# First loads, tanh and constants as ordered steps, and all orders laid down anew, in a two-layer gated cross-attention and mixture-of-experts kernel

## The reference

```python
x = x + tanh(g_xattn[0]) * L0_xattn(layernorm(x), ctx_768, ...)   # 8 heads of 64, softmax over 512 keys
x = x + tanh(g_ffn[0])   * L0_ffn(layernorm(x), ...)              # 16 heads of 8 over 256 keys + top-2 of 8 experts
x = x + tanh(g_xattn[1]) * L1_xattn(layernorm(x), ctx_768, ...)   # 16 heads of 8, softmax over 512 keys
x = x + tanh(g_ffn[1])   * L1_ffn(layernorm(x), ...)              # router, top-2 of 8 experts
```

## Time and profile before

| | before |
|---|---|
| median of 3 timed runs | 726.27 us (725.82 to 726.75) |
| the profiled execution | 733.98 us, span 732.2 us |
| mean granted clock of PE | 0.968 |
| busy share of PE, DVE, ACT, POOL | 91%, 70%, 55%, 53% |

### The profile page before, as it was taken

How to read it: one execution, slowest core, us unless ns; L and a number is a source line. 1 busy time by engine, 2 the same in 40 slices (tenths; PEclk the granted TensorE clock), 3 DMA queues, 4 the chain that set the end, 5 groups by cost and what they waited for, 6 DMA issues and landing times.

```text
span 732.2 us, 14403 instructions
## 1 busy us (share of the span) xinstructions
PE 666.7 (91%) x5766; PEld 347.3 (47%) x5766; DVE 515.4 (70%) x1018; ACT 402.4 (55%) x574; POOL 385.8 (53%) x535
## 2 busy tenths in 40 slices
PE   6898998998989899988999998999999999999984
PEld 4454554543445454543445454546445543544542
DVE  2505658698558965778868889777479979957636
ACT  1464556446734676426673586476744666376540
POOL 5465675781454547563538746573648625234041
PEclk9899999999898999989999999999999989999998
DMA  6040400511091010820145124240060031000000
GB/s 179 22 95 5 101 3 9 119 24 45 10 161 34 2 45 9 168 33 3 46 99 104 54 51 86 56 99 10 1 130 26 20 78 45 1 20 8 2 1 15
DMA packets 58338, 36.92 MB, mean 50 GB/s; under 512 B 4984, under 2 KB 56288, under 8 KB 58272
## 3 DMA queue, kind: packets, MB, share of 16 engines
q1 hardware_dynamic: 57728, 35.74, 22.2%
q10 hardware_dynamic: 544, 0.26, 0.1%
HBM read 21.07 MB, written 14.93 MB: 49 GB/s over the span
## 4 chain that ended last, share of the span: by engine, by line
PE 53%; DVE 26%; ACT 6%; POOL 5%; DMA 4%; issue 3%; SPq 1%; DVEq 0%; POOLq 0%; ACTq 0%
PE psum L878 7%; PE psum L730 6%; PE psum L743 5%; DVE mx8B L1225 5%; DVE mx8F L1220 5%; PE psum L834 5%; PE psum L866 4%; DVE mxA L1105 3%; PE psum L847 2%; PE psum L702 2%; PE psum L803 2%; PE psum L708 2%; ACT probB L996 2%; PE psum L815 2%; PE psum L761 1%
## 5 line engine op out<-in xcount | busy, mean ns | idle before, releaser
L1225 DVE TENSOR_REDUCE mx8B<-psum 128x2 f32<-128x1024 f32 x112 | 131.6, 1216 | 15.1 <-PE psum L847 14.2
L996 ACT ACTIVATE probB<-psum 128x1024 f32<-128x1024 f32 x112 | 110.7, 1028 | 25.5 <-PE psum L866 19.9
L953 ACT ACTIVATE probX<-psum 128x1024 f32<-128x1024 f32 x64 | 65.5, 1023 | 54.8 <-PE psum L734 54.2
L1105 DVE TENSOR_REDUCE mxA<-psum 128x2 f32<-128x1024 f32 x64 | 76.5, 1217 | 25.2 <-PE psum L714 24.9
L1220 DVE TENSOR_REDUCE mx8F<-psum 128x4 f32<-128x1024 f32 x56 | 66.2, 1219 | 21.9 <-PE psum L841 21.5
L730 PE MATMUL psum<-qA,kA 64*128 64x256 f32 x512 | 76.9, 393 | 1.0 <-ACT mrow L926 0.5
L996 ACT ACTIVATE probF<-psum 128x1024 f32<-128x1024 f32 x56 | 56.7, 1026 | 21.1 <-PE psum L866 17.8
L743 PE MATMUL psum<-probX,vX 128*64 128x256 f32 x512 | 63.8, 393 | 0.7 <-ACT probX L953 0.3
L1316 POOL TENSOR_TENSOR prodC<-prodC 128x256 f32<-128x256 f32 x28 | 20.3, 727 | 73.7 <-DVE prodC L1197 73.7
L878 PE MATMUL psum<-probB,v8B 128*9 128x256 f32 x896 | 56.0, 392 | 0.3 <-ACT probB L996 0.2
L1292 POOL TENSOR_TENSOR sums<-probX 128x512 f32<-128x512 f32 x32 | 40.6, 1267 | 21.4 <-ACT probX L953 21.3
(11 more groups left out here) (254 smaller groups left out, 1368.0 us busy)
## 6 DMA issues: line engine op xcount, KB each, us to landing
k8B<-k_dK SPq DMA_DIRECT2D x14, 384.0 KB, 6.8
k_dK<-partsK SPq DMA_DIRECT2D x7, 384.0 KB, 2.6
q8F<-q_dF SPq DMA_DIRECT2D x14, 192.0 KB, 4.3
k8F<-k_dF SPq DMA_DIRECT2D x14, 192.0 KB, 5.0
q8B<-q_dB SPq DMA_DIRECT2D x14, 192.0 KB, 4.0
k_dK<-partsK SPq DMA_DIRECT2D x7, 256.0 KB, 2.9
cTX<-in_ctxT SPq DMA_DIRECT2D x8, 192.0 KB, 2.6
cTK<-in_ctxT SPq DMA_DIRECT2D x8, 192.0 KB, 2.5
```

The lines of the kernel that those rows point to most:

```text
L953: nc.scalar.activation(prob[s][k % SLOTS[s]][:], ps, ACT.Exp, scale=float(XD) ** -0.5).then_inc(done["ACT"], 1)
L996: nc.scalar.activation(prob[s][(units * b + k) % SLOTS[s]][:], ps, ACT.Exp, scale=float(D8) ** -0.5).then_inc(done["ACT"], 1)
L1105: nc.vector.tensor_reduce(mxA[:, t, h:h + 65:64], ps.rearrange("p (i n) -> p i n", i=2), AX.X, ALU.max, negate=True).then_inc(drained, 1)
L1225: nc.vector.tensor_reduce(mx8[s][:, t, 2 * p:2 * p + 2], ps.rearrange("p (i n) -> p i n", i=2), AX.X, ALU.max, negate=True).then_inc(drain ...
```

## The change

The 25 loads that SP issued ahead of its list become steps `("X", "ld", 0, k)`, so that the table orders them among `xin` and `ctx`. The gates move from ACT's queue to SP's, and `wqx` and `wvx` from SP's to ACT's. The tanh becomes the step `th` of ACT's list. The two masked biases leave `sets` and become a step of their own, `bm`, with a semaphore of its own (`b_set`), for which only the steps of the last batch element wait. The planner's figures change: an entry of SP's queue now lands no earlier than those ahead of it have been served (`SERVE`), and no filler matmul is planned ahead of 12 us on its own clock (`FILL_FROM`). All five strings are new. The number of filler matmuls falls from 15 to 6; the rest of the instructions is the same.

```diff
-START = {"PE": 5.4, "DVE": 5.2, "ACT": 5.0, "POOL": 1.3, "SP": 9.0}
+START = {"PE": 5.4, "DVE": 5.2, "ACT": 4.0, "POOL": 1.3, "SP": .75}
+LOADS, FIRST_LOADS, LANDED = 25, 5, 9
+SERVE = {"sr": {"F": 4.6, "K": 5., "B": 2.2}, "sw": {"F": 2.6, "K": 2.1, "B": 1.3}, "ctx": {"X": .9, "K": .9}}
+FILL_FROM = 12.
...
-    "POOL": "dacebalffffffffggehijfafffjffffjjkggehlimajfnojffjfjffffkggheimjjjjkonfalfpfffffqqfqmggheqriojjfpnffjfjffakfflqq"
+    "POOL": "abdcmfgggaggggghhfimjgkggagkggkggklhhfijngapkkggkgkgglggohhfijknakkpgeklggggqogggmrhhifrnrjrspkqkgaoggkgggggrklm"
...
+    if b == 0:
+        for k in range(LOADS):
+            p.job("SP", "X", "ld", b, k, .46)
     plan_norm(p, "X", b, [("SP", "X", "xin", b, 0)], [("PE", "X", "qp", b - 1, 0)])
     if b == 0:
         p.job("POOL", "X", "pick", b, 0, 1.1)
-        p.job("POOL", "X", "bo", b, 0, 1.3)
+        p.job("ACT", "X", "th", b, 0, .2, ("SP", "X", "ld", 0, LANDED + 1))
+        p.job("POOL", "X", "bo", b, 0, 1.3, ("ACT", "X", "th", b, 0), ("SP", "X", "ld", 0, LANDED + 3))
         p.job("POOL", "K", "sets", b, 0, 9.8)
+        p.job("POOL", "F", "bm", b, 0, .65, ("SP", "X", "ld", 0, LOADS - 1))
...
+                if e == "SP" and key[2] != "ld":
+                    served = over[key] = max(over[key], served + SERVE.get(key[2], {}).get(key[1], .35))
...
-        warm[fill] = int(min(20, max(0., idle - IDLE) // WARM_UP)) if WARM else 0
+        warm[fill] = int(min(20, max(0., idle - IDLE) // WARM_UP)) if WARM and start > FILL_FROM else 0
...
+        first = [(loaded["graw"], graw[:, 0:2], a["g_xattn"].rearrange("(o n) -> o n", o=1).broadcast_to([P, 2])),
+                 (loaded["graw"], graw[:, 2:4], a["g_ffn"].rearrange("(o n) -> o n", o=1).broadcast_to([P, 2])),
+                 (loaded["bo"], bo["X"][:], a["boX"].rearrange("(o n) -> o n", o=1).broadcast_to([P, P])),
+                 (loaded["bo"], bo["B"][:], a["boB"].rearrange("(o n) -> o n", o=1).broadcast_to([P, P])),
+                 (loaded["wox"], wox[:], a["wox"])]
+        loads = first + [(w_loaded, dst, src) for dst, src in loads]
...
-            load_ctx("X", 0)
-            load_x(0)
-            engine.dma_start(wqx[:], a["wqx"]).then_inc(loaded["wqx"], 16)
-            engine.dma_start(wvx[:], a["wvx"]).then_inc(loaded["wvx"], 16)
...
+                elif name == "ld":
+                    which, dst, src = loads[k]
+                    engine.dma_start(dst, src).then_inc(which, 16)
...
-            act.wait_ge(loaded["graw"], 32)
-            nc.scalar.activation(gates[:], graw[:], ACT.Tanh).then_inc(tanh_done, 1)
+            engine.dma_start(wqx[:], a["wqx"]).then_inc(loaded["wqx"], 16)
+            engine.dma_start(wvx[:], a["wvx"]).then_inc(loaded["wvx"], 16)
...
+                if name == "th":
+                    act.wait_ge(loaded["graw"], 32)
+                    nc.scalar.activation(gates[:], graw[:], ACT.Tanh).then_inc(tanh_done, 1)
+                    continue
...
-                    act.wait_ge(k_set, K_SETS)
+                    act.wait_ge(b_set, 2)
...
+                elif name == "bm":
                     pool.wait_ge(w_loaded, W_LOADS)
                     for to, n in (("F", 0), ("B", 2)):
-                        engine.tensor_scalar(bqm[to][:], mask[:], bqn[:, n:n + 1], None, ALU.mult).then_inc(k_set, 1)
+                        engine.tensor_scalar(bqm[to][:], mask[:], bqn[:, n:n + 1], None, ALU.mult).then_inc(b_set, 1)
```

More of the change, by code:

```diff
@@ L133, in plan_x @@
 def plan_x(p, b):
-    p.job("SP", "X", "xin", b, 0, .4 if b else 0., ("DVE", "X", "xh", b - 1, 0), ("POOL", "X", "xb", b - 1, 0))
-    p.job("SP", "X", "ctx", b, 0, .4 if b else 0., ("PE", "X", "kp", b - 1, 1), ("PE", "X", "vp", b - 1, 1))
+    p.job("SP", "X", "xin", b, 0, .4, ("DVE", "X", "xh", b - 1, 0), ("POOL", "X", "xb", b - 1, 0))
+    p.job("SP", "X", "ctx", b, 0, .4, ("PE", "X", "kp", b - 1, 1), ("PE", "X", "vp", b - 1, 1))
+    if b == 0:
+        for k in range(LOADS):
+            p.job("SP", "X", "ld", b, k, .46)
     plan_norm(p, "X", b, [("SP", "X", "xin", b, 0)], [("PE", "X", "qp", b - 1, 0)])
@@ L270, in plan_k @@
     for k in range(2):
-        p.fill("DVE", 0, "K", "vv", b, k, .45, .33, [("SP", "K", "ctx", b, 0)], [("PE", "B", "pv8", b - 1, 3), ("POOL", "K", "sets", b, 0)])
+        p.fill("DVE", 0, "K", "vv", b, k, .45, .33, [("SP", "K", "ctx", b, 0), ("SP", "X", "ld", b, LOADS - 1)], [("PE", "B", "pv8", b - 1, 3), ("POOL", "K", "sets", b, 0)])
 def plan_b(p, b):
@@ L304, in slack @@
 def slack(key):
+    if key[:3] == ("SP", "X", "ld"):
+        return 4. * (key[4] == LOADS - 1)
     if key in (("SP", "X", "xin", 0, 0), ("SP", "X", "ctx", 0, 0)):
-        return 0.
+        return 4.
     return OUT if key[0] == "PE" else LAND[key[1:3]] if key[0] == "SP" else 0.
@@ L341, in schedule @@
     bank_free, bank_of, held = [0.] * BANKS, {}, [None] * BANKS
-    mode = 0
+    mode, served = 0, 0.
     over, before, warm = {}, {}, {}
@@ L575, in build @@
                       (we[s][:].rearrange("p (e n) -> p e n", e=NE), a["we" + s].rearrange("e k n -> k e n"))]
-        bias = [(bo[n][:], a["bo" + n].rearrange("(o n) -> o n", o=1).broadcast_to([P, P])) for n in "XB"]
-        W_LOADS = 16 * len(loads)
-        X_SETS, K_SETS = 3, 7
+        first = [(loaded["graw"], graw[:, 0:2], a["g_xattn"].rearrange("(o n) -> o n", o=1).broadcast_to([P, 2])),
[4 more added lines that the diff above has]
+        loads = first + [(w_loaded, dst, src) for dst, src in loads]
+        assert len(loads) == LOADS and len(first) == FIRST_LOADS
+        W_LOADS = 16 * (LOADS - FIRST_LOADS)
+        X_SETS, K_SETS = 3, 5
         FIRST_STAGES = "X"
@@ L623, in load_parts @@
                             .then_inc(S[s]["sr"], 16)
-            load_ctx("X", 0)
-            load_x(0)
-            engine.dma_start(wqx[:], a["wqx"]).then_inc(loaded["wqx"], 16)
-            engine.dma_start(wvx[:], a["wvx"]).then_inc(loaded["wvx"], 16)
-            for dst, src in bias:
-                engine.dma_start(dst, src).then_inc(loaded["bo"], 16)
-            engine.dma_start(wox[:], a["wox"]).then_inc(loaded["wox"], 16)
-            for dst, src in loads:
-                engine.dma_start(dst, src).then_inc(w_loaded, 16)
             for s, name, b, k in ORDER["SP"]:
-                if name == "xin" and b > 0:
+                if name == "xin":
                     load_x(b)
-                elif name == "ctx" and (s, b) != ("X", 0):
+                elif name == "ctx":
                     load_ctx(s, b)
+                elif name == "ld":
+                    which, dst, src = loads[k]
+                    engine.dma_start(dst, src).then_inc(which, 16)
                 elif name == "tw":
```

55 lines of the change are left out of this document (27 added, 28 removed), and 18 rows, old and new, of the table STEPS.

## The result

| | before | after |
|---|---|---|
| median of the timed runs | 726.51 us (725.82 to 726.87, 4 runs) | 704.48 us (703.31 to 705.31, 4 runs) |
| ratio to before, 95% interval | | 0.9697 (0.9679 to 0.9715) |
| profiled execution, span | 733.98 us, 732.2 us | 705.11 us, 703.3 us |
| mean granted clock of PE | 0.968 | 0.982 |

The changed kernel is 3.0% faster. 711 us was forecast with a range of 699 to 720, so the time lies inside. The two steps of the sum do not hold: the start gave 1.3 us and not 10.3, and the rest gave about 21 and not 5.4.

What follows compares the result with a forecast made beforehand. PE, busy 91% of the span, was taken as the bound. 733.98 less 10.3 at the start and 5.4 from the other orders gave 718.3, times 0.9895 made 711 us, range 699 to 720.

Steps and rivals of the forecast that it cites:

- Step 1: Kernel start: POOL's statistics and PE's transposes go first, fills later; first exponent scores at 28.2 instead of 38.46, 10.3 us saved.
- the cover: Kernel start: work counted at no cost, such as POOL's 9.5 us of fills, run from about 8 to near 18.
- The chain behind the normalisation: Kernel start: transposes through at 8.6, key projection 12.3, query projection 14.7, first maximum 17.4, exponent scores 28.2.
- Step 2: Orders after the start: three PE waits for transfers go, 8.1 us idle less one new wait of 2.7, so 5.4 us.
- a new wait of their mean size: After the start: the new order was assumed to make one PE wait of 2.7 us, deducted from 8.1.
- these three places: PE's transfer waits near 181, 218 and 315 us: 1.31, 3.54 and 3.28 us idle, to be removed by reordering SP's queue.
- the first rival: Stretches near 181, 218 and 315: full clock returns once transfer waits go, another 10.2 us; 698 us, chance 0.20.
- The factor 0.9895: Whole kernel: median of three timed runs, 726.27, over the profiled 733.98; scales 718.3 to 711 us.
- The start's gain does not arrive: Kernel start: POOL's set-up or a first load is late, cancelling the gain, the rest even; about 726 us, chance 0.03.
- the forecast's own band: Whole kernel: measured time of 704 to 714 us, given chance 0.50.
- The clock comes back: Stretches near 181, 218 and 315: removing transfer waits also returns 10.2 us of half clock; 698 us, chance 0.20.
- the signs of being wrong: Profile after: first eviction waits for tanh, first key projection for context, or SP stands for an output before a reload.

## Why the prediction was right or wrong

- **The bound.** PE was and is the bound; that held.
- **Step 1, 10.3 us.** The trace gave 1.3 (0.5 against the second trace of before). The step that failed is the cover: POOL's fills, from about 8 to about 18, were counted at no cost. They hold DVE's normalisation until 17.56, so that it takes 10.56 where the sum had 0.65. No row was given for that nothing, and two rows of before seemed to allow it: DVE's statistics of 5.73 ran in 0.25 while POOL was filling, and the normalisation of 19.40 beside POOL's biases took 0.65. The first is another kind of instruction, and the second was beside other work. The view of the tile in the trace before had a warning in it that the prediction did not use, instructions of one form with a largest time of four times the least:

```profile
L1073 DVE TENSOR_SCALAR xhX<-xin,mvX,rstdX x16: 331/368/1427, 19.4 to 457.4; 128x128 f32<-128x128 f32 x16
L1087 DVE TENSOR_SCALAR xhX<-xin,mvX,rstdX x16: 336/1283/10490, 7.2 to 474.9; 128x128 f32<-128x128 f32 x16
```

The second row is the changed kernel's. Its median of 1283 says that later batches are held too, by one sum of POOL at a time (the one of 46.00 for 1.28 us, beside a sum of 45.93 to 47.20). That is part of the rest of DVE's 26 us more; PE waited for only one of these, 0.2 us.

- **The chain behind the normalisation** was right: with the fills away it gives the queries' end 14.7 (14.7), the first maximum 17.16 (17.4), the exponent scores 28.00 (28.2). The transposes were through at 9.2 (8.6), since the selector held the normalisation too (1.31 us); but the key projection began at 9.02, ahead of their modelled end, so that the queries began at 12.43 (12.3). The keys took 3.62, as at half clock, and the queries 2.26, near the 1.99 of full clock, so the clock rose soon after 12.43 (11.7 to 13.9). The tanh (5.49), the context and POOL's set-up (0.23 for the first operation, begun 0.17 behind the statistics) cost nothing, as taken.
- **Step 2, 5.4 us.** It is 20.7 by the medians (22.0 less 1.3), 18.6 to 27.6 by the traces. The waits for transfers did go, 7.7 us (3.9 to 11.5) with SP's order alone, which cannot be told from the 5.4; that a new wait of their mean size would come back was wrong, the longest in the changed kernel behind the start being 1.5. What failed is that the sum treated the new order as these three places: 8.6 us lie behind them all, in fewer waits for ScalarE, fewer falls of the clock and fewer changes of tile shape. Some 4 us more (22.0 less 1.3, 7.7 and 8.6), ahead of the third wait, are put down to nothing here.
- **The clock.** Taking nothing for it was wrong for the profiled pair. Between these two 10.3 us of half clock went, as the first rival had it; but the first trace of before was an execution with 13.7 us of it, where the next one had 5.1, which leaves 1.7. What went in the usual execution lies between the two and stays open. SP's order alone brought 7.7 (3.9 to 11.5), which the idle time alone can explain (8.1 by the first trace, 5.2 by the second). The factor 0.9895 in the sum carried this, without saying why.
- **The rivals.** "The start's gain does not arrive" had 0.03, and its first half is what happened, by a mechanism it did not name; its second half, that the rest is even, did not. The time lies at the edge of the forecast's own band (704 to 714), next to that of "The clock comes back", for the reason of neither. One of the signs of being wrong did show: in the changed kernel SP stood 2.6 us for the output of batch 0, until 287.19, with a reload of stage F's queries directly behind it. PE waited for no transfer there, so it cost nothing.

```profile
SPq L677 <- POOL accC L1364: 2.6, 1, 2.6
```

- **The number.** 711 against 704.5 came from two errors of opposite sign, 9 us too much at the start and 15 too little behind it. That the time lies in the range is luck.

## What to carry to other kernels

Before long fills on POOL are called free, look at what DVE does in that time: here one-input float32 arithmetic from on-chip memory to on-chip memory waited for them (10.56 us for two instructions), a reduction from PSUM (1.16 each) or a pair of instructions with two inputs (0.50) did not wait for a fill, and one wait in POOL's queue was enough to let DVE in. A new order is worth more than the waits one can name: add up idle time, half clock and busy time over a stretch with the same matmuls. And take a second trace, and the granted clocks of the timed executions, before the falls of the clock in the first are counted as a cost.

## What was not expected of the hardware

- Six of POOL's instructions without a wait between them kept DVE's one-input arithmetic out for all of them, 9.4 us beyond the instruction that was running; with a wait behind each, the first pause, of 0.06 us, ended it.
- A wait of PE for a transfer varies by execution with nothing changed: 1.3 and none at 181, 3.3 and 1.6 at 315, 3.5 and 3.6 at 218.
- A wait of 1.31 us had half clock behind it; in the changed kernel one of 1.1 near 182 had none, the granted clock of 180 to 200 being 1.00.
- A change of tile shape costs 0.10 to 0.12 us of PE in this kernel, by 62 changes more and 28 fewer.
